# Context of a two-layer cross-attention kernel split once per batch element, with keys and Gram products taken from the split parts

## What is computed

```python
# layer 0: 77 text tokens and 298 others, two attentions with their own softmax
out = attend(q, text @ Wk.T, text @ Wv.T) + attend(q, ip @ Wk_ip.T, ip @ Wv_ip.T)
x1  = out @ Wo.T + bo + x
# layer 1: 371 text tokens and 4 others
probs_t = softmax(q @ k_t * scale)              # k_t = text @ W_k
text_out = probs_t @ v_t
qsem  = l2norm(probs_t @ text)                  # 512 long, for each head and row
fused = q @ k_ip * scale + 0.5 * (qsem @ l2norm(ip))
out   = text_out + (softmax(fused) * spatial_mask) @ v_ip
x2    = out @ W_out + b_out + x1
```

## Time and profile before

| what | us |
|---|---|
| median of 3 runs (lowest, highest) | 2675.04 (2674.85, 2680.46) |
| the profiled execution | 2677.45 |
| its span in the trace | 2675.6 |

### The profile page before, as it was taken

One profiled execution on the slowest core, in us unless ns is written; L12 is line 12 of the kernel. 1 busy time (PEld: TensorE's weight loads), 2 busy tenths in 40 slices (PEclk: granted clock), 3 DMA queues, 4 the chain that ended last, 5 costly groups with the idle time before them and its releaser, 6 DMA issues.

```text
span 2675.6 us, 62303 instructions
## 1 busy us (share of the span) xinstructions
PE 2543.2 (95%) x25256; PEld 2027.5 (76%) x25256; DVE 1736.2 (65%) x3340; ACT 1248.8 (47%) x2301; POOL 808.6 (30%) x993
## 2 busy tenths in 40 slices
PE   5799999999999999999999999999999999999986
PEld 4577777777777777777787777777777777777774
DVE  2356677666677666677666677666676666677655
ACT  1344444544444554444554444544444544444543
POOL 1122333332333323333322333322333332333322
PEclk8899999999999999999999999999999999999997
DMA  8755666745566655566655566745676655567630
GB/s 182 121 90 89 93 92 89 102 88 88 84 94 89 108 85 84 84 94 99 97 84 86 83 105 85 105 76 91 90 92 89 98 82 88 83 91 97 89 37 7
DMA packets 493222, 241.37 MB, mean 90 GB/s; under 512 B 259628, under 2 KB 492924, under 8 KB 492925
## 3 DMA queue, kind: packets, MB, share of 16 engines
q1 hardware_dynamic: 477094, 214.33, 57.0%
q10 hardware_dynamic: 15840, 23.04, 2.9%
HBM read 171.35 MB, written 64.59 MB: 88 GB/s over the span
## 4 chain that ended last, share of the span: by engine, by line
PE 76%; DVE 17%; DMA 3%; issue 2%; SPq 1%; ACT 1%; POOL 0%; DVEq 0%; ACTq 0%; POOLq 0%
PE R L597 11%; PE ST L698 7%; DVE w L834 5%; PE PN L715 5%; PE R L742 5%; PE R L642 4%; DVE m L926 4%; PE R L655 4%; PE R L656 4%; PE R L598 4%; PE PN L759 3%; PE R L798 3%; PE R L658 3%; DVE w L831 3%; PE R L666 2%; PE R L745 2%
## 5 line engine op out<-in xcount | busy, mean ns | idle before, releaser
L1143 ACT ACTIVATE p<-ST 128x1344 f32<-128x1344 f32 x320 | 413.4, 1292 | 119.6 <-PE ST L701 115.7
L1270 POOL TENSOR_TENSOR w<-w 128x448 f32<-128x448 f32 (+1 forms) x256 | 330.1, 1289 | 443.4 <-DVE w L831 424.9
L834 DVE SCALAR_TENSOR_TENSOR w<-p,pr 128x1344 f32<-128x1344 f32 x160 | 315.8, 1974 | 170.6 <-ACT pr L1158 158.1
L831 DVE TENSOR_TENSOR rem<-R,kst 128x298 f32<-128x298 f32 (+2 forms) x184 | 91.4, 497 | 482.7 <-ACT kst L1038 482.7
L742 PE MATMUL R<-pr,Gh 128*128 128x448 f32 (+1 forms) x960 | 370.3, 386 | 0.3 <-issue 0.3
L1206 POOL TENSOR_TENSOR kst<-rem,kst 128x298 bf16<-128x298 f32 (+2 forms) x184 | 150.7, 819 | 615.9 <-ACT kst L1038 343.8
L655 PE MATMUL R<-wvh,ch 128*128 128x320 f32 (+3 forms) x896 | 303.3, 339 | 8.0 <-DVE cl L831 7.7
L597 PE MATMUL R<-cT,wk 128*128 128x298 f32 (+1 forms) x960 | 303.3, 453 | 7.9 <-DVE rem L831 7.7
L831 DVE TENSOR_TENSOR w<-R,w 128x448 f32<-128x448 f32 (+1 forms) x480 | 275.7, 617 | 45.1 <-PE R L747 37.7
L656 PE MATMUL R<-wvh,cl 128*128 128x320 f32 (+3 forms) x896 | 279.4, 312 | 0.0
L698 PE MATMUL ST<-Qs,Ks 100*128 100x112 bf16 (+1 forms) x3520 | 230.3, 214 | 16.3 <-DMA Qs<-ms 8.2
(11 more groups left out here) (173 smaller groups left out, 5430.6 us busy)
## 6 DMA issues: line engine op xcount, KB each, us to landing
Ks<-k_split SPq DMA_DIRECT2D x384, 140.6 KB, 6.0
Ks<-k_split SPq DMA_DIRECT2D x384, 93.8 KB, 8.2
Qs<-q_split SPq DMA_DIRECT2D x384, 70.0 KB, 8.4
cT<-in_ctxT ACTq DMA_DIRECT2D x30, 750.0 KB, 4.6
k_split<-kst SPq DMA_DIRECT2D x64, 281.2 KB, 3.4
k_split<-kst SPq DMA_DIRECT2D x64, 223.5 KB, 2.8
q_split<-qst SPq DMA_DIRECT2D x128, 84.0 KB, 2.2
k_split<-kst SPq DMA_DIRECT2D x64, 111.8 KB, 2.6
```

The costliest lines, as they stand in the source:

```text
L831: return e.tensor_tensor(to, x, y, op)
L834: return e.scalar_tensor_tensor(out=to, in0=x, scalar=s, in1=y, op0=op0, op1=op1)
L1143: e.activation(p32[i][:].rearrange("p (u q) -> p u q", u=3), st, ACT.Exp).then_inc(p_whole, 1)
L1270: e.tensor_tensor(first, first, w2[n % 2][0:ROWS[j], QW * j:QW * j + QW], ALU.add).then_inc(ns_added, 1)
```

## The change

The parts of the context are made once for each element, for all 375 tokens, into `ch[b % 2]` and `cl[b % 2]` (376 columns now). Values, keys of the 298 and 371 tokens, and Gram products read them; the raw context is no longer kept. It is loaded into the memory of `w2` (for element 0 of `pvt`), by SyncE instead of ScalarE. The key weights get two parts at the start of the kernel. V1 and w2 hold raw key weights for a while, so some loads and a memset move; the scratch of the program's own DMA is made smaller.

```diff
     def values(todo):
...
-                if t == 2 and b + 2 < B:
-                    o.add("ctx", b + 2, "act")
+                    o.add("split", b + 2)
...
+        if b + 2 < B:
+            o.add("ctx", b + 2)
         count = [0]
         rows0 = iter(())
...
# tensor, keys of layer 0's 298 and layer 1's 371 tokens
+                        i, t0, t1 = (1, 0, TEXT1 + 1) if l == 1 else (0, TEXT0, T)
+                        h, lo, wh, wl = ch[b % 2], cl[b % 2], wkh[i], wkl[i]
+                        w.wait_ge(c_low, 4 * (b + 1))
+                        w.wait_ge(wk_low, i + 1)
+                        free(w, "R", ("k",) + key)
+                        for k in range(4):
+                            e.matmul(r[:, 0:t1 - t0], wh[:, k, c0:c0 + 128], h[:, k, t0:t1], start=k == 0, stop=False)
+                            e.matmul(r[:, 0:t1 - t0], wh[:, k, c0:c0 + 128], lo[:, k, t0:t1], start=False, stop=False)
+                            if k < 3:
+                                e.matmul(r[:, 0:t1 - t0], wl[:, k, c0:c0 + 128], h[:, k, t0:t1], start=False, stop=False)
...
# tensor, Gram
-                    c, n, first = cT[b % 2], ROWS[t], min(128 * t, T - 128)
+                    h, lo, n, first = ch[b % 2], cl[b % 2], ROWS[t], min(128 * t, T + 1 - 256)
...
-                    for k in range(3):
-                        e.matmul(r[0:n, first:T], c[:, k, 128 * t:128 * t + n], c[:, k, first:T], start=k == 0, stop=False)
+                    for k in range(4):
+                        hk, lk = h[:, k, 128 * t:128 * t + n], lo[:, k, 128 * t:128 * t + n]
+                        e.matmul(r[0:n, first:T + 1], hk, h[:, k, first:T + 1], start=k == 0, stop=False)
+                        e.matmul(r[0:n, first:T + 1], hk, lo[:, k, first:T + 1], start=False, stop=False)
+                        mm = e.matmul(r[0:n, first:T + 1], lk, h[:, k, first:T + 1], start=False, stop=k == 3)
...
# scalar
+                elif kind == "split":
+                    b, = key
+                    w.wait_ge(d_ctx[b % 2], 16 * (b // 2 + 1))
+                    w.wait_ge(c_pads, 1)
+                    if b >= 2:
+                        w.wait_ge(g_mm, at("g", b - 2, 2))
+                    for k in range(4):
+                        copy(ch[b % 2][:, k, 0:T], context(b)[:, k, :]).then_inc(c_hi, 1)
...
# gpsimd
+                elif kind == "split":
+                    b, = key
+                    for k in range(4):
+                        w.wait_ge(c_hi, 4 * b + k + 1)
+                        less(cl[b % 2][:, k, 0:T], context(b)[:, k, :], ch[b % 2][:, k, 0:T].bitcast(fp32)).then_inc(c_low, 1)
...
# sync
+                    if b == 1:
+                        w.wait_ge(wv_low, 1)
+                    elif b:
+                        w.wait_ge(c_low, 4 * b)
+                        if b > 2:
+                            w.wait_ge(ns_mm, NG * (b - 2))
+                    e.dma_start(context(b), a["ctxT"][b].rearrange("(k e) t -> e k t", e=128)).then_inc(d_ctx[b % 2], 16)
...
# vector, before it writes w2
+                    w.wait_ge(c_low, 4 * min(B, (k - 1) // NG + 3))
```

More of the change, by code:

```diff
@@ L54, in stage_order @@
     later = []
-    tile, uses = [0], [0]
+    uses = [0]
     def in_bank(what, signal, value):
@@ L256, in stage_order @@
     o.add("load", 1)
+    o.add("split", 0)
+    o.add("key_weights", 0)
     keys(0, "t", 0)
@@ L284, in stage_order @@
     o.add("weights", 0)
-    ip_values = values([(0, 0, t) for t in range(3)])
-    next(ip_values)
+    o.add("split", 1)
     def with_maxima():
         yield text_values(0)
-        yield from ip_values
+        yield from values([(0, 0, t) for t in range(3)])
     start = with_maxima()
@@ L878, in vector @@
                     e.tensor_copy(V0[:, 0, :, D:FV0], mip[:].unsqueeze(1).to_broadcast([128, H, 1])).then_inc(v_mask, 1)
+                elif kind == "key_weights":
+                    i, = key
+                    w.wait_ge(wk_hi, i + 1)
+                    tt(wkl[i][:], wkraw[i], wkh[i][:].bitcast(fp32), ALU.subtract).then_inc(wk_low, 1)
                 elif kind == "weights":
@@ L886, in vector @@
                     w.wait_ge(d_vw, 16)
[L887 to L894, removed]
-                            w.wait_ge(v_mm, user_of_parts[j - 2])
-                        e.tensor_copy(h, c).then_inc(dve_step, own.one())
-                        w.wait_ge(dve_step, own.n)
-                        tt(lo, c, h.bitcast(fp32), ALU.subtract).then_inc(parts_dve, 1)
                 elif kind == "g":
@@ L1081, in scalar @@
                     w.wait_ge(wv_low, 3)
[L1082 to L1089 removed]
+                    w.wait_ge(d_vw, 16)
                 elif kind == "v":
@@ L1215, in gpsimd @@
                 elif kind == "start":
+                    for i in range(2):
+                        e.memset(ch[i][:, :, T:T + 1].bitcast(fp32), 0.0)
+                        c_zeros = e.memset(cl[i][:, :, T:T + 1].bitcast(fp32), 0.0)
+                    c_zeros.then_inc(c_pads, 1)
                     for t_ in Ks:
@@ L1315, in sync @@
                     elif key[0] == 2:
+                        w.wait_ge(wk_low, 1)
+                        load("wv0")
                         w.wait_ge(kip_mm, 3)
```

158 lines of the change are left out of this document (58 added, 100 removed).

## The result

| what | before | after |
|---|---|---|
| median of the runs, us (lowest, highest) | 2677.64 (2674.85, 2680.46) | 2613.89 (2613.34, 2614.57) |
| the profiled execution | 2677.45 | 2613.9 |
| its span in the trace | 2675.6 | 2612.1 |

The ratio is 0.9762, with a 95% interval of 0.9745 to 0.9779: faster by about 64 us. The forecast was 2617 with a range of 2594 to 2650. A second measurement of the changed kernel, beside the last experiments, gave 0.9755 (0.974 to 0.9769).

The account below looks back on a forecast made before the run. TensorE, 76% of the chain, was taken as the bound except where VectorE (17%) holds it. Per pass -2.47 + 0.29 + 0.2 = -1.98, times 31 = -61, with +5 and -1.6: -58, forecast 2617 us, range 2594 to 2650.

Parts of the forecast that it names:

- What bounds the kernel: Whole kernel: TensorE's savings count, except where VectorE holds the chain, from 1320.99 to 1338.18 us; key tiles are on the path.
- Keys: Key tiles in groups0: 12 float32r matmuls replace 8 fp32 instructions, three 298-wide and two 371-wide tiles, -2.47 us a pass.
- Gram: Gram tiles: tile 0's 0.47 saving uncounted under VectorE, tile 1 -0.25, tile 2 +0.54; counted +0.29 us a pass.
- Parts off VectorE: Groups0 and start of groups1: VectorE loses two 0.928 us differences and their casts a pass; counted as nothing.
- Hand-over: End of the maxima: split of b + 2 makes groups0's first exponential late, +0.2 us a pass, bounds 0 and +1.2.
- Load: Load of b + 2 moved to SyncE's queue lands before the split needs it: nothing, bound +0.5.
- Start: Kernel start: split(1) waits for its load, +4 us, bounds 0 and +10; key-weight splits +1; together +5.
- End: Kernel end: the 1.60 us TensorE waited for the last element's parts goes away, -1.6 us.
- 1: All matmuls: passes cost the same in fp32 and float32r, 298 wide 0.131 us; -2.61 a pass, 2597 us; chance 0.14.
- 2: End of the maxima: the hand-over costs 1.2 us a pass instead of 0.2, giving 2648 us; chance 0.16.
- 3: Key and Gram tiles: narrow float32r matmuls are charged like fp32 ones, slower, about 2825 us; chance 0.05.
- 4: Groups0: shorter key tiles leave TensorE waiting for ScalarE's exponentials, no change, about 2675 us; chance 0.03.

Follow-up runs that it names:

- experiment 1: Changed kernel with the keys as fp32 matmuls of the high parts only, low parts left out: 2672.11 us, ratio 0.997 to the kernel before.
- Experiment 2: Changed kernel with Gram products as fp32 matmuls of the high part only, 375, 247 and 128 wide: 2608.43 us, ratio 0.9728 to the kernel before.
- experiment 3: Changed kernel with Gram tiles 1 and 2 in float32r 248 and 120 columns wide instead of 256: 2605.8 us, ratio 0.9732 to the kernel before.
- experiment 4: Changed kernel with three unused 256-column differences on VectorE where the second pair of context parts stood: 2632.82 us, ratio 0.9824 to the kernel before.
- experiment 5: Kernel before, with only the second pair of context parts of each pass moved from VectorE to ScalarE and GpSimd: 2665.47 us, ratio 0.995.
- experiment 8: Changed kernel with element 1's split moved behind the first value tiles and first maxima: 2607.57 us, ratio 0.9726 to the kernel before.
- Experiment 7: Changed kernel with only the first of GpSimd's four differences of each split made twice: 2639.24 us, ratio 0.986 to the kernel before.
- experiment 6: Changed kernel with each of GpSimd's four differences of the split made twice: 2787.49 us, ratio 1.0405 to the kernel before.

## Why the prediction was right, and where its steps were off

**What bounds the kernel.** The chain is not on VectorE all the way from 1320.99 to 1338.18, as the prediction reads it: TensorE holds it from 1328.10 to 1330.97. Gram tile 0 stands behind that, so nothing in the sum hangs on it. Right for groups0: TensorE is busy 22.46 of 22.46 us, and the keys' type, by itself, is worth 1.93 us a pass (experiment 1). It was incomplete for the first groups of groups1. The chain gives them to TensorE, but one of its pieces there is longer than its neighbours only because VectorE was late (0.46 us where they have 0.20, above), so work on VectorE "some 15 us ahead of the point where VectorE takes over" did cost time.

**Keys**, -2.47 a pass: mis-sized. The prices per matmul held (0.140 for 0.137, 0.170 for 0.169). The count of 12 equal matmuls per tile did not: the first takes 0.22 and 0.25 us, 0.08 more than the others. The fp32 price was an average over a tile and already held what its first matmul costs (by the single records the first instruction of a 298-wide fp32 tile behind scores takes 0.31 us, each in the row behind it 0.25); the float32r price came from value tiles that follow other float32r matmuls. Five tiles make 0.4 us, and with the 0.003 us per matmul the term measured -1.94: 16 us too much over 31 passes.

The last matmul of a tile takes 0.09 more where products of layer 0 stand behind it, in both types, and the new tiles start up to 0.07 us sooner behind the matmul in front of them. From the matmul in front to the one behind, the three 298-wide tiles are 0.34 to 0.35 us shorter each and the two others 0.44 and 0.45, 1.93 in all. Why the first costs more was not tried. The rows fit a weight load with no long matmul in front of it: the last score matmul starts only 0.03 us ahead of the key tile.

**Gram**, +0.29 counted: right. Experiment 2 gives +0.27, experiment 3 puts 0.29 on the widening alone. The first matmul of a Gram tile takes 0.25 us in place of 0.12, but starts 0.13 sooner behind the one in front. But the maxima as a whole did not get longer: about 0.3 us a pass came back. 0.17 of it is one small operation of VectorE, on the chain, that stood beside a difference of GpSimd in the kernel before (L834 into fus, 0.47 us at 1336.75, as in 29 of the 32 elements) and takes 0.30 now in all of them. The rest I did not place. I had no term for either.

**Parts off VectorE**, counted at nothing: the step that failed by sign. The first pair is nothing, as said. The second is worth 0.45 us a pass, 13.5 us in all, shown from both sides (experiment 4: +0.64 in groups1, experiment 5: -0.48). The sentence "between them it waits for ScalarE's exponentials anyhow" looked at VectorE's idle time in sum; but the pair stood in front of the product that GpSimd's sums wait for, and pushed those sums onto the next pass over w2. In the pass shown that makes 0.64 us of the 0.76 by which this pass over w2 ends later (measured from the start of the one before it); no run takes the overlap away and leaves the delay, so this split of the cause rests on the timeline.

**Hand-over**, +0.2: it was 0, the lower bound. GpSimd took 3.56 us where the 371-wide row had given 3.7, and ended by 1332.1, 0.66 us before the first scores, where the forecast had 0.4 (1355.2 against 1355.6). The three copies behind it took 1.1 us and not 1.23. The order of the events was as described, up to ScalarE's waits.

**Load**, 0: right in the passes; the split never waits for it there. **Start**, +5: it was +11 in the profiled execution. There the load was issued at 67.9 instead of 66.1, and ScalarE's copy of the landed data began at 76.57, 8.7 us after the issue began, where I had taken 4.6 from a median of the quiet passes; it shares the DMA engines with the loads of the weights (their busy share is about 1.0 from 60 to 75 us). TensorE stood 12.62 us for the text values behind it. With the +1 for the weights that is the far end of the bounds I gave; the changed kernel measured again has +6, and others with the same start up to +17 (experiment 8). That experiment puts 0.37% on the place of the split. **End**, -1.6: -2.0.

In sum: keys 16 us short, the start 6 worse; against that groups1 14, the maxima 9 (0.29 x 31) and the hand-over 6 better. The forecast of -58 met -63.5 partly by luck: errors of both signs cancelled.

**Rivals.** 1: wrong, the passes cost 0.140 and not 0.131 at 298 columns, and an fp32 instruction in the middle of its row costs 0.25, so half of one is 0.125. The rule of four passes for fp32 (the Trainium skill, page "FP8 and Floating Point Precision", section "TensorE Precision Notes") against three is right in kind, but by it alone the keys would have gained 2.86 a pass and gained 1.94. 2: its mechanism is real and its price was a little high. Experiment 7 adds 1.06 us and loses 0.85, so differences as slow as the 476-wide one (1.1 us more) would have cost about 0.9 us a pass; it did not happen because GpSimd kept to the 371-wide price. 3: refuted (experiment 3). 4: refuted, no wait of TensorE in groups0.

## What to carry to other kernels

An engine with idle time can still be on the path: ask of each instruction that is taken off it what stands right behind it, and whose start that sets, not how idle the engine is on average. When a tile's price is moved from one type to another, take the whole slot from the matmul before it to the one behind it; a price from the middle of a long row of equal matmuls leaves out the first one. Where a chain ends just in time, as the split does here with 0.2 us to spare, the next microsecond on it costs nearly all of itself, and a wait of 3.5 us on TensorE may cost more than its length.

## What the runs showed of the hardware that was not expected

- Float32r matmuls with their own weights each: 0.100 us at 120 columns, 0.114 at 248, 0.119 at 256, 0.140 at 298, 0.170 at 372. Narrow ones are not charged like fp32, but at 120 columns the price is above the line of the wide ones (0.06). The first of a tile behind bf16 matmuls takes 0.08 (keys) to 0.13 (Gram) more. fp32 in the middle of a row takes 0.25 per recorded instruction at 298 columns and 0.31 at 371, so two float32r matmuls of that width are dearer than one such instruction, by about a tenth.
- VectorE's pass over w2 (two inputs in SBUF, 1344 columns) takes 1.56 us alone and 2.20 beside a sum of GpSimd, and about 1.1 us of other work on VectorE, placed badly, brings them together.
- With a wait of 3.5 us in each pass the granted clock was at one half for a part of groups0 in 29 of 30 passes and full in one (experiment 6); with a gap of 0.9 us (experiment 7) groups0 has the same length in every pass of its kind.
